# A two-layer transformer block on one core: the first batch is projected straight into its score strips, and the loads of the ramp are reordered

## The reference

```
qkv = x @ Wqkv + bqkv                       # 16 heads of 8 features
q, k, v = split(qkv.reshape(bs, 256, 16, 24), 3)
scores = einsum('bqhd,bkhd->bhqk', q, k) / sqrt(8)
out = einsum('bhqk,bkhd->bqhd', softmax(scores), v) @ Wproj + bproj
x = layernorm(x + out)
```

## Time and profile before

| | us |
|---|---|
| median of three runs | 377.0 (376.42 to 378.9) |
| the profiled execution's own time | 378.37 |
| its span, from the first to the last instruction | 376.6 |
| TensorE busy in the span | 341.9 |
| mean granted TensorE clock | 0.97 of full |

### The profile page before, as it was taken

How to read it: one execution, slowest core, us unless ns; L and a number is a source line. 1 busy time by engine, 2 the same in 40 slices (tenths; PEclk the granted TensorE clock), 3 DMA queues, 4 the chain that set the end, 5 groups by cost and what they waited for, 6 DMA issues and landing times.

```text
span 376.6 us, 10486 instructions
## 1 busy us (share of the span) xinstructions
PE 341.9 (91%) x3912; PEld 239.6 (64%) x3912; DVE 238.1 (63%) x907; ACT 203.9 (54%) x439; POOL 170.8 (45%) x284
## 2 busy tenths in 40 slices
PE   3989999999989999899998899799899999999872
PEld 2557666665648556575567666488677777777652
DVE  3365566577758577376764738548597878883354
ACT  2015666665694656746574545834665565656310
POOL 7036964020202502346143766616958685453621
PEclk9998999999999999899998989969999999999998
DMA  4493150101010101101111001110111111000000
GB/s 146 63 293 58 35 138 3 30 3 30 3 30 2 31 3 31 29 3 30 30 31 28 21 13 30 30 28 4 44 32 44 31 44 30 18 3 17 2 15 29
DMA packets 9219, 14.04 MB, mean 37 GB/s; under 512 B 2001, under 2 KB 4945, under 8 KB 9041
## 3 DMA queue, kind: packets, MB, share of 16 engines
q1 hardware_dynamic: 8656, 13.11, 15.1%
q10 hardware_dynamic: 512, 0.26, 0.4%
HBM read 5.76 MB, written 1.05 MB: 18 GB/s over the span
## 4 chain that ended last, share of the span: by engine, by line
PE 79%; POOL 6%; DVE 5%; ACT 4%; issue 3%; DMA 2%; POOLq 0%; DVEq 0%; ACTq 0%
PE SM L292 27%; PE G L479 13%; PE ST L311 6%; PE G L389 5%; PE G L376 4%; PE G L365 4%; PE G L447 3%; PE G L348 3%; PE G L355 3%; PE G L398 2%; PE G L461 2%; POOL QK L815 2%; PE G L415 2%; DMA QK<-mt 2%; PE ST L453 1%
## 5 line engine op out<-in xcount | busy, mean ns | idle before, releaser
L535 ACT ACTIVATE E<-ST 128x512 f32<-128x512 f32 (+1 forms) x256 | 125.4, 541 | 89.0 <-PE ST L311 88.8
L311 PE MATMUL ST<-QK 32*128 32x256 f32 (+1 forms) x1024 | 138.5, 380 | 9.6 <-ACT E L535 8.0
L292 PE MATMUL SM<-QK 31*128 31x256 f32 (+1 forms) x1024 | 140.2, 379 | 0.8 <-DVE mx L668 0.7
L292 PEld LDWEIGHTS SM<-QK 31*128 31x128 f32 x1024 | 93.3, 186 | 40.5 <-DVE mx L668 13.2
L668 DVE TENSOR_REDUCE mx<-SM 128x2 f32<-128x512 f32 x128 | 82.2, 685 | 56.5 <-PE SM L292 56.3
L311 PEld LDWEIGHTS ST<-QK 32*128 32x128 f32 x1024 | 91.8, 187 | 14.1 <-ACT E L535 9.9
L676 DVE CUSTOM_DVE_ANT_0 masked_s<-SM,mask_sb 128x256 f32<-128x256 f32 (+1 forms) x256 | 75.7, 351 | 36.2 <-PE SM L292 35.9
L824 POOL TENSOR_SCALAR_AFFINE_SELECT E<-E 128x512 f32<-128x512 f32 x64 | 39.1, 634 | 43.5 <-ACT E L535 43.5
L479 PE MATMUL G<-E,V 128*32 128x256 f32 x992 | 53.6, 356 | 0.0
L479 PEld LDWEIGHTS G<-E,V 128*32 128x32 f32 x992 | 28.4, 109 | 20.3 <-issue 4.6
L777 POOL TENSOR_SCALAR nm_a<-mv_a 128x2 f32<-128x2 f32 x15 | 2.9, 193 | 62.7 <-DVE mv_a L635 62.7
(11 more groups left out here) (135 smaller groups left out, 453.8 us busy)
## 6 DMA issues: line engine op xcount, KB each, us to landing
QK<-qk SPq DMA_DIRECT2D x62, 64.0 KB
rs<-ry SPq DMA_DIRECT2D x16, 128.0 KB, 2.3
xb<-x_nat SPq DMA_DIRECT2D x1, 1024.0 KB, 8.1
out<-ln_g SPq DMA_DIRECT2D x8, 128.0 KB, 2.0
xt<-x_t SPq DMA_DIRECT2D x1, 896.0 KB, 6.7
wi<-wi_all SPq DMA_DIRECT2D x1, 576.0 KB, 4.9
QK<-mt SPq DMA_DIRECT2D x32, 8.0 KB
fac<-fac_u SPq DMA_DIRECT2D x1, 508.0 KB, 4.6
```

The source lines that it names most:

```text
L292: ins = nc.tensor.matmul(SM[m % S_RING][:, cols], q, QK[rows, b % QK_RING, r, 1, keys], start=True, stop=True)
L311: ins = nc.tensor.matmul(ST[m % S_RING][:, c * T:(c + 1) * T - q0], QK[rows, b % QK_RING, r, 1, c * P:(c + 1) * P], QK[rows, b % QK_RING, ...
L535: act.activation(E[:, a % E_RING, j, 0:n], ST[m % S_RING][:, 0:n], ACT.Exp, scale=SCALE)\
```

## The change

It touches the steps up to g = 4 and the place of the loads; from then on each engine has the same instructions in the same order, but for the loads of `late`, which come a step later.

- New weights `wfirst` (128 inputs by 4 groups by 2 by 128) have the columns of q and k already at their strip rows, with zeros elsewhere; a bias `bfirst` adds the ones. One pair of matmuls and two evacuations fill one group of QK's slot 0 without a DMA. Group 0 is in step -34, groups 1, 2 and 3 are in steps -12, -8 and -4, after the scores of the step.
- Batch 1 is projected in step -10 (before: -18) and batch 2 in step 2 (before: -2). The four strip DMAs of batch 1 are issued from ScalarE's queue; before, SP issued them.
- A zeroed tile `idle`, set by VectorE as its first instruction, feeds the three 128x512 matmuls, which now come ahead of everything else on TensorE. GpSimd zeroes three slots instead of four.
- `filler` runs only for the last 8 heads ahead of 0 (FILL), in steps -8 to -2.
- SP issues 15 loads at the start, then the ones, and then waits for the first `mt`. Of `late`, `xb` (1 MB) comes first, in step -2.
- VectorE makes `bv_all` in step -2 instead of at the start.

```diff
-AT_QK, AT_QKIN, AT_ROPE = -34, (-32, -24), -28
+AT_QK, AT_QKIN, AT_ROPE = -34, -24, -28
...
-BXU, BXD, TURN, JOIN, BV, XB_AT, WF_AT, LATE = (4, 6), 16, 32, 22, 0, 14, 38, -20
+BXU, BXD, TURN, JOIN, BV, XB_AT, WF_AT, LATE = (4, 6), 16, 32, 22, 0, 14, 38, -2
...
+FIRST_AT, EARLY, FILL = (FIRST, -12, -8, -4), (None, -10, 2), 8
...
+def projected_at(g):
+
+    if g in EARLY:
+        return EARLY.index(g)
+    b = batch_at(g, AT_QK)
+    return b if b is not None and b >= len(EARLY) else None
...
         def _(sp):
             sp.dma_start(xt[:, 0:T], x_t[:, 0:T]).then_inc(ld["x0"], 16)
+            sp.dma_start(wqk_sb[:, :, :], wqk0).then_inc(ld["qk"], 16)
+            sp.dma_start(bqk_sb[:, :], bqk0).then_inc(ld["qk"], 16)
+            sp.dma_start(xt[:, T:TOK], x_t[:, T:TOK]).then_inc(ld["x"], 16)
             sp.dma_start(id32[:, :], ident).then_inc(ld["id"], 16)
-            sp.dma_start(xt[:, T:TOK], x_t[:, T:TOK]).then_inc(ld["x"], 16)
             sp.dma_start(wv_sb[:, :], wv0).then_inc(ld["v"], 16)
...
+            for loaded, dst, src in loads:
+                sp.dma_start(dst, src).then_inc(loaded, 16)
+            for b in range(1, QK_RING):
+                sp.wait_ge(zeros_ready, b)
+                sp.dma_start(QK[MAXROW:P:STRIP, b, :, 1, :], ones).then_inc(ones_in[b], 16)
...
             for g in STEPS:
...
+                if (n := half_at(g - 2, AT_MT)) is not None:
+                    b, t = divmod(n, 2)
+                    sp.wait_ge(A["mt_ready"], n + 1)
+                    sp.dma_start(QK[MAXROW:P:STRIP, b % QK_RING, 2 * t:2 * t + 2, 0, :], mt[:, n % 2, :]).then_inc(m_in[n % 4], 16)
...
                 if c == 1:
-                    if m % H == 0:
-                        pe.wait_ge(qk_in[b % QK_RING], 16 * STRIPS * (b // QK_RING + 1))
+                    if b == 0 and j == 0:
+                        pe.wait_ge(first_out, 2 * (r + 1))
+                    elif m % H == 0:
+                        pe.wait_ge(qk_in[b % QK_RING], 16 * STRIPS * loads_of(b))
...
-                        elif -LEAD <= m < 0:
+                        elif -FILL <= m < 0:
                             filler(m, long)
+
+
+            pe.wait_ge(idle_ready, 1)
+            for i in range(S_RING):
+                nc.tensor.matmul(ST[i][:, :], idle[:, 0:P], idle[:, :], start=True, stop=True)
 
             for g in STEPS:
                 scores(g)
+
+                for r in range(GROUPS):
+                    if g == FIRST_AT[r]:
+                        bank = claim(("first", r), first_out, 2 * (r + 1))
...
+                        for s in range(2):
+                            ins = nc.tensor.matmul(bank[:, s * T:(s + 1) * T], wfirst_sb[:, r, s, :], xt[:, 0:T], start=True, stop=True)
+                        ins.then_inc(first_ps, 1)
...
         def _(act):
-            act.dma_start(wqk_sb[:, :, :], wqk0).then_inc(ld["qk"], 16)
-            act.dma_start(bqk_sb[:, :], bqk0).then_inc(ld["qk"], 16)
-            act.dma_start(bv_sb[:, :], bv0).then_inc(ld["bvc"], 16)
+            act.dma_start(wfirst_sb[:, 0, :, :], wfirst[:, 0, :, :]).then_inc(ld["first"], 16)
+            act.dma_start(bfirst_sb[:, :, :], bfirst).then_inc(ld["first"], 16)
+            act.dma_start(wfirst_sb[:, 1:GROUPS, :, :], wfirst[:, 1:GROUPS, :, :]).then_inc(ld["groups"], 16)
...
+                for r in range(GROUPS):
+                    if g == FIRST_AT[r]:
+
+                        act.wait_ge(first_ps, r + 1)
+                        if r == 0:
+                            act.wait_ge(ld["first"], 32)
+                        for s in range(2):
+                            act.activation(QK[:, 0, r, s, :], g_bank["first", r][:, s * T:(s + 1) * T], ACT.Identity,
+                                           bias=bfirst_sb[:, r, s:s + 1]).then_inc(first_out, 1)
...
-                        if b == 0:
+                        if b == 1:
                             act.wait_ge(A["qk_out"], 2)
                             act.wait_ge(zeros_ready, 1)
-                            for j in range(2, STRIPS):
-                                act.dma_start(QK[STRIP * j:STRIP * j + ROWS, 0, :, :, :], qk[j:P:STRIPS, 0, :, :]).then_inc(qk_in[0], 16)
+                            for j in range(STRIPS):
+                                act.dma_start(QK[STRIP * j:STRIP * j + ROWS, 1, :, :, :], qk[j:P:STRIPS, 1, :, :]).then_inc(qk_in[1], 16)
```

More of the change, by code:

```diff
@@ L88, in sem @@
             return ctx.enter_context(nc.semaphore(name))
+        wfirst_sb = sb("wfirst_sb", [P, GROUPS, 2, W])
+        bfirst_sb = sb("bfirst_sb", [P, GROUPS, 2])
+        idle = sb("idle", [P, 512])
         wqk_sb = sb("wqk_sb", [P, 2, W])
@@ L154, in block_kernel @@
         G = [ctx.enter_context(nc.psum_tensor(f"G{i}", [P, 512], F32)) for i in range(2)]
-        ld = {n: sem(f"ld_{n}") for n in ("x0", "x", "qk", "v", "id", "bf", "up", "bv", "bvc", "xb", "proj", "l1", "next", "rope", "gate")}
+        ld = {n: sem(f"ld_{n}") for n in ("x0", "x", "first", "groups", "qk", "v", "id", "bf", "up", "bv", "bvc", "xb", "proj", "l1", "next", "rope", "gate")}
         zeros_ready, v_clean, half_ready = sem("zeros_ready"), sem("v_clean"), sem("half_ready")
@@ L302, in exp_scores @@
                         pe.wait_ge(m_in[n % 4], 16 * (n // 4 + 1))
[L303 removed]
+                    if m % H == 0 and 0 < b < QK_RING:
                         pe.wait_ge(ones_in[b], 16)
@@ L448, in _ @@
                     ins.then_inc(A["qk_ps"], 1)
-                if g == FIRST:
-                    pe.wait_ge(zeros_ready, QK_RING)
-                    for i in range(3):
-                        nc.tensor.matmul(ST[i][:, :], QK[:, QK_RING - 1, 0, 0, 0:P],
-                                         QK[:, QK_RING - 1, 0, :, :].rearrange("p s t -> p (s t)"), start=True, stop=True)
                 if (b := batch_at(g, AT_V)) is not None:
@@ L636, in statistics @@
                 ins.then_inc(var_ready, 1)
+            nc.vector.memset(idle[:, :], 0.0).then_inc(idle_ready, 1)
             def normalise_last(N, parity, ln_ready):
@@ L755, in _ @@
                         normalise_last(NA, b % 2, A["ln_ready"])
+                if g == BV - 2:
+                    dve.wait_ge(ld["id"], 16)
+                    dve.wait_ge(ld["bvc"], 16)
+                    nc.vector.tensor_scalar(bv_all[:, :], id32[:, :], 0.0, bv_sb[:, 0:1], ALU.mult, ALU.add).then_inc(bv_ready, 1)
                 if g == BV:
@@ L813, in _ @@
             nc.gpsimd.memset(half[:, :], -0.5).then_inc(half_ready, 1)
-            for i in range(QK_RING):
+            for i in range(1, QK_RING):
                 nc.gpsimd.memset(QK[:, i, :, :, :], 0.0).then_inc(zeros_ready, 1)
@@ L967, in _arrays @@
     kcol = [2 * D * (h // rep) + 2 * d, 2 * D * (vh // rep) + 2 * vd + 1]
+    wfirst, bfirst = np.zeros((P, GROUPS, 2, P), np.float32), np.zeros((P, GROUPS, 2), np.float32)
+    bfirst[MAXROW::STRIP, :, 1] = 1.0
+    for s, cols in enumerate((q, k)):
+        for i, c in enumerate(cols):
+            row, head = divmod(i, H)
+            to = STRIP * (head % STRIPS) + row
+            wfirst[:, head // STRIPS, s, to], bfirst[to, head // STRIPS, s] = wqkv[:, c], bqkv[c]
     u = np.concatenate([a["L0_ffn_W_exp"].T, a["L0_ffn_b_exp"][:, None]], 1)
```

89 lines of the change are left out of this document (44 added, 45 removed).

## The result

The changed kernel takes 382.85 us (median of four, 381.67 to 383.51) against 377.95 us (376.42 to 379.58) for the kernel before on the same chip: ratio 1.0109, 95% interval 1.0071 to 1.0148. It is slower by 1.1%, and lies outside the forecast's range. Measured once more (twelve runs against 29) the ratio was 1.0073, interval 1.0037 to 1.0108. Medians are of all executions; ratios and their intervals leave out those more than 1.5% above the fastest of their kernel. The profiled execution took 383.0 us.

The account below looks back on a forecast made before the run. TensorE, busy 91% of the span, was taken as the bound, so only the ramp up to step 4 counted: -4.6 + 4.2 - 0.6 + 1.3 = +0.3 us, median 377.3 us, range 373.8 to 381.0.

Parts of the forecast that it names:

- A: Kernel start to first scores on TensorE: they start at 9.4 us instead of 13.97, 4.6 us gained (3.8 to 5.5).
- B: First scores (S) to first exponential score (X) on TensorE: 18.0 to 19.1 us instead of 14.3, 4.2 lost.
- Rival 1: Ramp: ScalarE's DMA issues do not hold up group 2's evacuation; -2.8 us, so 374.2; chance 0.14.
- C: First exponential score to step 4: 4.2 us with batch 2's projection instead of 4.83, 0.6 gained.
- D: TensorE's clock in the new ramp: one low stretch of 3.4 us over steps -6 and -4, 1.3 lost (0 to 1.7).
- Rival 2: TensorE stays at its lower clock through most of the ramp, costing 5.4 instead of 1.3: 381.4 us; chance 0.14.
- Rival 3: Ramp: the maxima's DMA stays late behind 3.5 MB of early loads; +1.5 us more, 378.8; chance 0.06.

Follow-up runs that it names:

- e2_after_cover: Changed kernel with one more 128x512 matmul on the idle tile behind each group's projection; 379.19 us, ratio 0.9975 to the kernel before.
- e2_after_sp_cover: Changed kernel with batch 1's strip DMAs issued by SP and one idle matmul behind each group's projection; 375.15 us, ratio 0.9915 to the kernel before.
- after: Changed kernel as it is, first trace; profiled execution 383.0 us, median 382.85 us, ratio 1.0109 to the kernel before.
- e1_after: Changed kernel, unchanged, for a second trace and more executions; 382.10 us, ratio 1.0073 to the kernel before.
- e1_after_plus1: Changed kernel with one more unread 128x512 matmul behind the scores of step 4; 382.09 us, ratio 1.0089 to the kernel before.
- e3_after_holes: Changed kernel with unread matmuls covering TensorE's waits behind step 4; 376.53 us, ratio 0.9903 to the kernel before.
- e1_before_plus2: Kernel before with two more unread 128x512 matmuls behind the scores of step 4; 381.72 us, ratio 0.9996 to the kernel before.
- e1_before: Kernel before, unchanged, one execution for a second trace; 376.54 us.
- before: Kernel before the change, first trace; profiled execution 378.37 us, median 377.95 us beside the changed kernel.
- e3_before_holes: Kernel before with unread matmuls covering TensorE's waits behind step 4; 371.60 us, ratio 0.9815 to the kernel before.
- e2_after_fill14: Changed kernel with FILL at 14, so fillers also in steps -14, -12 and -10; 382.88 us, ratio 1.0076 to the kernel before.

## Why the prediction was wrong

By its own steps, on the first trace of the changed kernel where no other is named:

- **A, the first scores.** 4.6 us expected, 5.2 found (8.80 for 13.97). VectorE was free at 0.96 and not at 1.51 us, so all of TensorE's start moved by half a microsecond. Right, a little small.
- **B, the ramp at full pace.** 18.0 to 19.1 us from S to X. `e2_after_cover`, which has full pace, took 19.3: 5.0 us more than before, for the 4.2 of the sum (3.7 to 4.8). ScalarE's four issues took 3.17 us, between the two prices I had (2.62 and 3.76), and head 8, VectorE and the transpose waited behind them as said. The mechanism is right, the size 0.8 us too small. Rival 1 is out: with the strips issued from SP as well (`e2_after_sp_cover`) the same stretch took 17.3 us, so the issues on ScalarE are worth 2.0 us of the ramp at full pace. The Trainium skill (DMA: Bandwidth & Descriptors, section "Issuing engines are not separate DMA queues") calls that part "usually small relative to the DMA itself"; the trace does not agree here, with 3.17 us for four issues, 0.79 each, where a whole transfer takes 2.3.
- **C, from X to step 4.** 34.16 - 29.98 = 4.18 against 4.2.
- **D, the clock in the ramp. This is the step that failed.** I expected one low stretch of 3.4 us behind the hole ahead of head 8, worth 1.3. The low stretches of the ramp were 6.8, 10.2, 6.8 and 13.7 us in the four traces with this ramp (`after`, `e1_after`, `e1_after_plus1`, `e3_after_holes`). In the first three they began ahead of that hole, in the steps without fillers: in the hole of 0.93 us behind group 1's projection, and in the second trace in the 0.78 us in which head 3 waits for the first maxima. In the fourth the fall came where I had put it, and lasted four times as long. From S to X these traces took 21.2, 23.1, 21.2 and 22.1 us for the 19.3 of full pace: 1.9 to 3.8 us for D's 1.3 (0 to 1.7). Rival 2, which I gave 0.14, comes nearest. Its place, the steps ahead of step -8, fits three of the four; but in those three the clock rose again before step -4, which it had excluded, and its 5.4 us were not reached.
- **The baseline.** I had taken the low stretch at 29.7 us for a property of the kernel before. It is one of two outcomes: step 4 starts at 33.07 us in the trace with it and at 30.77 in one without. Against the latter the changed ramp loses 3.4 us (first trace) and 5.4 us (second), not the 1.1 of the first pair. The 1 us that the range had for the scatter of medians was short as well: the kernel before ran over 6 us from one execution to the next, and its medians went from 377.0 us (three executions) to 379.04 (31).
- **Behind step 4** I said nothing comes of the change. With the holes covered the traces bear that out: the distance of the maxima's transposes is 3.1 us from step 10 to the last one. The medians of that set are 4.9 us apart, and the difference is explained for the traced pair only. In the first pair of traces 3.2 us came from a fall that one execution had and the other not.
- **Rival 3** did not happen: the maxima's DMA was issued at 24.81 and not waited for.

So the sum was +0.3 us and should have been: A -5.2 + B 5.0 - C 0.6 + D 1.9 = +1.1 on the first pair of traces, and +3.4 to +5.4 against a trace of the kernel before without a fall. The medians say +3.2 (378.93 to 382.10) and +4.9 (first set). A slip in the range changes nothing in this: 377.0 - 2.4 is 374.6, not 374.8. That the change loses because the direct projection puts ScalarE and its DMA issues between TensorE's scores, and because TensorE's clock then falls, is shown by the two edits that mend each; why the clock falls at one hole and not at another is not shown. That a version with the reordered loads alone gains 2.8 us is shown too, with the later holes covered; without the covers it was not run.

## What to carry to other kernels

Before a sum is made from one trace, look for low stretches of TensorE's clock in it, and ask of each whether it is the kernel's or that execution's: a second trace of the same kernel moved the baseline by 2.3 us here. A chain that is latency-bound on three engines is not shortened by starting it sooner if its links (project, evacuate, score) come one behind another; each hole it leaves on TensorE can be paid twice, once as a wait and once as clock. Where TensorE must wait for another engine for 1 to 3 us, matmuls that nothing reads, no longer than the wait, were worth 7.4 us (2%) in this kernel. Behind the first gelu they cost nothing: the transposes around that hole are 14.45 us apart with them and in the trace of before with full clock there (105.2 to 119.65). And a large load belongs behind the small transfer that the next step waits for.

## What the runs showed of the hardware

- A hole of 1.85 us at the same instruction, near 112 us, was followed by full clock in one execution of the kernel before and by 3.4 us at 1.2 GHz in the other, and in the changed kernel by 6.8 us in one and 3.4 in the other.
- The length of a hole alone does not say whether the clock falls. Ahead of X in the kernel before, holes of 1.30 and 1.35 us (`e1_before_plus2`, `e1_before`) were passed and holes of 1.64 and 1.76 us (`before`, `e3_before_holes`) were not. In the changed ramp the clock fell in holes of 0.78 and 0.93 us, and holes of 1.60, 2.03 and 2.44 us (`after`, `e2_after_cover`, `e1_after`) were passed at full clock.
- Once low, the clock can stay low on a busy engine: in `e2_after_fill14` it was at half for 17 us, with TensorE busy for 12.5 of the 14 us from 20 to 34, most of it in matmuls on strips of 31 or 32 rows. In the changed kernel it was at half from 15 to 20 us with TensorE busy all the time.
- The clock column shows full speed at the start of every trace, while matmuls of 128x512 come 0.85 us apart (six in 5.49 us, the idle tile); their durations tell the pace there, not the column.
- Four issues of a 64 KB strip DMA took 3.17 us on ScalarE's queue with SP's idle, and 2.62 us on SP's.
